# Two attention and expert layers on one core: the second layer's keys and values are projected during the first routing, its keys are split during the first experts, and the first attention masks and takes its row maxima on VectorE

## The reference

```python
x = x + attention(layernorm(x), ctx, ctx, mask, Wq, Wk, Wv, Wout, b_out, is_causal=1)
x = x + experts(layernorm(x), ...)            # 16 experts of width 512, the best 2 of each row
x = x + attention(layernorm(x), ctx, ctx, Wq, bq, Wk, bk, Wv, bv, Wo, bo)
x = x + experts(layernorm(x) * g + b, ...)    # 7 experts of width 1024, capacity 732, and a shared one

def attention(query, key, value, ...):        # 16 heads of 16 channels
    q, k, v = query @ Wq + bq, key @ Wk + bk, value @ Wv + bv
    scores = q @ k.T / 4                      # first layer only: causal and given mask set to -inf
    return softmax(scores) @ v @ Wo + bo
```

## Time and profile before

| | us |
|---|---|
| three runs | 1266.15, 1257.76, 1257.41 |
| median | 1257.76 |
| profiled execution: its time | 1257.77 |
| profiled execution: its span | 1256.0 |

### The profile page before, as it was taken

The page is one execution under the profiler, slowest core; times in us unless marked ns, Lnnn a source line. Parts: engine busy times, 40 slices in busy tenths (PEclk is TensorE's granted clock), DMA queues, the critical chain, the costliest instruction groups (busy, mean ns, idle before and its releaser), DMA issues. The chain is left out here.

```text
span 1256.0 us, 26319 instructions
## 1 busy us (share of the span) xinstructions
PE 1123.8 (89%) x8539; PEld 981.6 (78%) x8540; DVE 689.2 (55%) x1558; ACT 595.2 (47%) x1211; POOL 359.9 (29%) x502
## 2 busy tenths in 40 slices
PE   6999999729999984898998679999999999999997
PEld 4688787419999973565665379999999999999996
DVE  4755656562222236776776755555555555555556
ACT  3576666303233223776786344444444454444432
POOL 6556650112222215776531045000000000000251
PEclk9899999859999987999999779999999999999999
DMA  7775472665667848566580221223222232232132
GB/s 181 176 179 126 122 175 49 246 239 183 209 215 207 213 142 172 124 131 127 98 126 9 101 93 52 82 64 113 85 90 80 93 102 86 87 106 68 50 98 80
DMA packets 88713, 156.31 MB, mean 124 GB/s; under 512 B 11315, under 2 KB 60013, under 8 KB 87872
## 3 DMA queue, kind: packets, MB, share of 16 engines
q1 hardware_dynamic: 72288, 119.90, 36.5%
q0 software_dynamic: 9584, 29.32, 8.1%
q10 hardware_dynamic: 6768, 6.16, 1.5%
HBM read 116.86 MB, written 39.20 MB: 124 GB/s over the span
## 5 line engine op out<-in xcount | busy, mean ns | idle before, releaser
L2146 PE MATMUL e_ps<-xT_e,wp_e 128*128 128x384 f32 (+1 forms) x1344 | 245.2, 331 | 4.0 <-DVE wp_e L2020 4.0
L2146 PEld LDWEIGHTS e_ps<-xT_e,wp_e 128*128 128x128 f32 x1344 | 221.7, 188 | 5.4 <-issue 4.1
L640 DVE TENSOR_REDUCE att_ps<-att_ps 128x2 f32<-128x512 f32 (+1 forms) x224 | 155.2, 696 | 104.3 <-PE att_ps L987 64.5
L1978 ACT ACTIVATE act_a_e<-e_ps 128x256 f32<-128x256 f32 (+2 forms) x176 | 77.7, 442 | 159.0 <-PE e_ps L2146 153.9
L893 ACT ACTIVATE probs<-att_ps 128x384 f32<-128x384 f32 (+1 forms) x256 | 130.4, 546 | 43.2 <-PE att_ps L1019 28.9
L2076 DVE TENSOR_TENSOR hid_e<-act_a_e,e_ps 128x256 f32<-128x256 f32 (+2 forms) x176 | 86.9, 494 | 115.8 <-ACT act_a_e L1978 99.5
L1982 ACT ACTIVATE hidp_e<-hid_e 128x256 fp32r<-128x256 f32 (+2 forms) x176 | 83.8, 476 | 127.5 <-DVE hid_e L2076 119.7
L2163 PE MATMUL e_ps<-wp_e,hidp_e 128*128 128x256 f32 (+1 forms) x1008 | 138.4, 282 | 2.9 <-DVE xres L2036 1.2
L2078 DVE TENSOR_TENSOR hidp_e<-hid_e,hidp_e 128x256 fp32r<-128x256 f32 (+2 forms) x176 | 87.7, 498 | 95.4 <-ACT hidp_e L1982 91.6
L2163 PEld LDWEIGHTS e_ps<-wp_e,hidp_e 128*128 128x128 f32 (+1 forms) x1008 | 130.7, 183 | 4.9 <-issue 4.1
L1613 ACT ACTIVATE hid_e<-e_ps,b_ahead 128x128 f32<-128x128 f32 x188 | 53.6, 368 | 132.6 <-PE e_ps L1718 121.4
(11 more groups left out here) (236 smaller groups left out, 1855.1 us busy)
## 6 DMA issues: line engine op xcount, KB each, us to landing
w_e<-in_W SPq DMA_DIRECT2D x47, 512.0 KB
w_e<-in_W SPq DMA_DIRECT2D x57, 384.0 KB, 3.1
ks<-parts SPq DMA_DIRECT2D x96, 128.0 KB, 4.7
qs<-parts SPq DMA_DIRECT2D x96, 128.0 KB, 6.1
parts<-cut SPq DMA_DIRECT2D x30, 384.0 KB, 3.0
w_ahead<-in_W SPq DMA_DIRECT2D x4, 2048.0 KB, 17.9
x_e<-rows SPq DMA_DIRECT2D x8, 768.0 KB, 6.2
done<-y_e ACTq DMA_DIRECT2D x47, 128.0 KB, 1.9
```

Of the source, the lines that this page charges most:

```text
L640: dve.tensor_reduce(tops_at(at[3])[:, qt, x0:x0 + heads], src, AX.X, ALU.max).then_inc(reduced, 1)
L1978: act.activation(act_a[:, u % 2, 0:n], ps[:, AB + u % 2, 0:n], ACT.Silu).then_inc(silu_ready, 1)
L2146: last = pe.matmul(ps[:, bank + u % 2, 0:n], weights(lot, c, pw)[:, (b * DC + d) * P:(b * DC + d + 1) * P], xT[:, px, d, t0:t0 + n], start ...
```

## The change

Three parts.

1. **Attention 0.** `score` no longer adds the mask (8 matmuls a group fewer), and `scoreT` still does. On VectorE `reduce` becomes one `tensor_tensor_reduce` for each head: it adds the mask `shut` to the scores and takes the maximum of each row, 8 a group instead of 3 reductions; what it adds up is also written to a buffer that nobody reads. The maxima go to SBUF (`row_tops`), in both attentions. VectorE's loop over batches 1 to 4 is written out in attention 0.
2. **Keys and values of attention 1 for batches 2 to 7.** Routing 0 loads their context and the matrices, and projects batches 2, 3 and 4; experts 0 projects 5, 6 and 7, before and between its four lots and behind them. ScalarE takes each out of PSUM.
3. **Key parts.** GpSimd splits these keys during experts 0, one step between two gathers of rows, and stores the parts by its own DMA. In attention 1 batches 2 to 7 have no slots for keys and values, GpSimd splits queries only, and SP loads the key stack without a wait for a store and the query stack behind its own store. The loads `Wk`, `Wv` and `bk` go from experts 0 to routing 0.

The core of the diff:

```diff
+def project_early(pe, out, kv, f, kind, half):
+    ctx = kv["ctx"][:, f - OPENED]
+    for c in range(DC):
+        if kind == "k":
+            last = pe.matmul(out[:, half * S:(half + 1) * S], kv["wk"][:, c, half * P:(half + 1) * P], ctx[:, c, :], start=c == 0, stop=c == DC - 1)
+        else:
+            last = pe.matmul(out[:, half * D:(half + 1) * D], ctx[:, c, half * P:(half + 1) * P], kv["wv"][:, c, :], start=c == 0, stop=c == DC - 1)
+    return last
...
             def reduce(at, u):
                 qt, x0, heads = UNITS[u]
                 dve.wait_ge(scored, ready(group(at) * NU + u))
+                if causal:
...
+                    for x1 in range(heads):
+                        col = x1 * 512 // heads
+                        last = dve.tensor_tensor_reduce(out=closed_scores[:, qt, x0 + x1, 0:keys(qt)], in0=ps[:, unit_bank(at, u), col:col + keys(qt)],
+                                                        in1=shut[:, 0, at[0], qt, 0:keys(qt)], scale=1.0, scalar=MASKED, op0=ALU.add, op1=ALU.max,
+                                                        accum_out=tops_at(at[3])[:, qt, x0 + x1:x0 + x1 + 1])
+                    last.then_inc(reduced, 1)
+                    return
...
-                    last = pe.matmul(out, qs[0:KS, j, hd, qt * P:(qt + 1) * P], ks[0:KS, j, hd, 0:keys(qt)], start=True, stop=not causal)
-                    if causal:
-                        last = pe.matmul(out, m["identb"][:], closed(n, 0, qt, 0, keys(qt)), start=False, stop=True)
+                    last = pe.matmul(out, qs[0:KS, j, hd, qt * P:(qt + 1) * P], ks[0:KS, j, hd, 0:keys(qt)], start=True, stop=True)
...
             for f in range(FEED, B):
                 j = f % 2
                 for i, w in enumerate(KINDS):
-                    store(f, i, w)
+                    if not (kept and w == 1):
+                        store(f, i, w)
                 sp.wait_ge(scoredT, (f + 1) * H)
+                if kept:
+                    load_stack(sp, ks, j, parts_dram, 1, f, stacks_loaded[j])
+                    sp.wait_ge(parts_stored[j], stored_upto(f))
+                    load_stack(sp, qs, j, parts_dram, 0, f, stacks_loaded[j])
+                    continue
...
                 if fed(n):
-                    if ye is not None:
-                        split_stepwise(pool, f, 1)
-                    else:
+                    if not kept:
                         split(pool, f, 1)
...
+        IN_PICKS = ((2, "k", TB), (2, "v", TB + 1))
+        IN_RANKS = ((3, "k", WB), (3, "v", WB + 1), (4, "k", LB), (4, "v", LB + 1))
...
+                for c in range(DC):
+                    sp.dma_start(kv["ctx"][:, :, c, :], a["ctxT"][c * P:(c + 1) * P, OPENED * S:T].rearrange("p (f s) -> p f s", s=S)).then_inc(kv_loaded, 16)
+                for w in ("k", "v"):
+                    sp.dma_start(kv["w" + w][:], kv["W"]["W" + w].rearrange("(c p) n -> p c n", p=P)).then_inc(kv_loaded, 16)
...
-            for name in ("Wk", "Wv", "Wq", "Wo"):
+            for name in ("Wq", "Wo"):
...
             for n in range(NB0):
                 pool.wait_ge(turned, free(n))
                 pool.indirect_dma_start(x[:, n % RING], None, rows, bass.IndirectOffsetOnAxis(ap=owner[:, n:n + 1], axis=0)).then_inc(x_loaded[n % RING], 16)
+                k = n - RING
+                if 0 <= k < (B - OPENED) * (CUTS + 1):
+                    cut_keys(OPENED + k // (CUTS + 1), k % (CUTS + 1))
...
+            AT_LOT = (range(0, 4), range(4, 6), range(6, 7), range(7, 9))
             for k in range(2 * NT):
                 if k % MARKS == 0:
+                    for h in AT_LOT[k // MARKS]:
+                        make_half(h)
...
+            for h in range(AT_LOT[-1].stop, 2 * len(PIECES)):
+                make_half(h)
+            pe.wait_ge(kv_taken, len(PIECES) - 1)
```

More of the change, by code:

```diff
@@ L161, in attend_block @@
     biased = "bq" in W
+    kept = ye is not None
     ctx = ExitStack()
@@ L512, in values @@
             def values(n):
-                pool.wait_ge(v_taken, n + 1)
+                if not (kept and n >= FEED):
+                    pool.wait_ge(v_taken, n + 1)
                 if n >= 2:
@@ L795, in _ @@
                 split(dve, 1, 0)
-            batches(dve, batch)
+            if causal:
+                for n in range(B):
+                    batch(n, n % 2, n // 2, n == 0, n == B - 1)
+            else:
+                batches(dve, batch)
             normalize((B - 1, 1, None, NG - 1))
```

126 lines of the change are left out of this document (108 added, 18 removed).

## The result

The changed kernel takes 1250.3 us (median of six, 1244.75 to 1252.34), the kernel before, run beside it, 1259.2: a ratio of 0.993, with a 95% interval of 0.990 to 0.996. That is faster, but by 0.7% and not by the 2.4% predicted (1227.3 us), and above the range (1212 to 1248). The profiled execution took 1245.86 us, its span is 1244.2, against 1256.0 before.

The account below looks back on a forecast made before the run. It took TensorE to pace attention 0's projecting batches, with VectorE also near its limit in the last, and TensorE and GpSimd attention 1's. -7.5 - 21 - 3 + 1 = -30.5 us from 1257.77 gave 1227.3 us, range 1212 to 1248.

Parts of the forecast that it names:

- Attention 1, -21 us: Attention 1: without key and value projection and key split, batches come out at 20.8 us; -21 us (-25 to -15).
- Attention 0, -7.5 us: Attention 0: masks leave TensorE for VectorE's pairs; batches 1 to 5 save 9.5 us, batch 7 loses 2; -7.5 us.
- rival (b): Attention 0: VectorE's pairs are nearly free, 12 to 14 us gained; 1217 to 1222 us; chance 0.13.
- End of experts 0, -3 us: End of experts 0: three of eleven loads go, shortening TensorE's wait for weights and low clock; -3 us (-4 to -2).
- Routing 0 and start of experts 0, +1 us: Routing 0 and start of experts 0: twelve added 1.72 us pieces nearly fit idle time at full clock; +1 us (-1.5 to +8).
- rival (c): Routing 0: added pieces meet a low clock, its leave or the first lot waits, +8 us; 1234 us; chance 0.10.
- (d): Attention 1: query stacks stay its pace, a third of the 21 us or more is lost; 1235 to 1248 us; chance 0.08.
- (a): Attention 0: pairs cost VectorE the upper bound or more, gaining nothing or losing up to 6 us; 1234 to 1244 us; chance 0.20.

Follow-up runs that it names:

- e12: Changed kernel with a key split on parts nobody reads put back between last gather and bias in attention 1: 1254.1 us, ratio 0.994.
- e1: Changed kernel with GpSimd's roots and query split in attention 1 ordered by a semaphore instead of drains: 1240.9 us, ratio 0.987.
- e4: Kernel before with GpSimd's roots and query split in attention 1 ordered by a semaphore instead of drains: 1249.8 us, ratio 0.995.
- e5: Changed kernel with, in attention 1, GpSimd's roots and query split by semaphore and the row maxima in PSUM: 1237.0 us, ratio 0.985.
- e6: e5 with eight key matmuls put back in each feeding batch of attention 1, into a PSUM bank nobody reads: 1235.6 us, ratio 0.983.
- e2: Changed kernel with the row maxima of attention 1 back in PSUM, attention 0's still in SBUF: 1246.8 us, ratio 0.992.
- e14: Changed kernel with nothing else but the maxima of both attentions in PSUM: 1247.3 us, ratio 0.991.
- e9: Kernel before with unread matmuls around routing 0's last ranks and the lots, including six calls behind the last lot: 1258.6 us (one run).
- e13: e6 with VectorE's combines divided over groups 0 and 1 and attention 0's maxima in PSUM too: 1235.2 us, ratio 0.980.

## Why the prediction was wrong, step by step

**Attention 1, -21 us: wrong, 0 measured, and the whole miss.** Three sentences of that part fail.

- "GpSimd loses the key split ... 21.3 us a batch." The split was costed as work on a busy engine. It was the cover of a wait: GpSimd's drain doesn't end before its gathers have landed, and they land at the end of the stack loads. Measured, the batch of GpSimd is 26.1 to 26.2 us. The wait of 1.1 to 3.1 us at L393 was in the trace of before, directly below the rows that I cited the earlier trace rows, marked "issue"; I read it as a fixed cost:

```profile
542.29 0.18 POOL L393 CAST bits<-spread 128x2 f32<-128x2 int32 x1 [1.94 <-issue]
```

  e12 shows that 3.7 us of work more there are taken up by that wait (13.9 us of it become 3.1), e1 and e4 that the drains were the pace, worth 5.9 and 6.9 us of the stage.
- "TensorE needs 18.6 us a batch." True as a sum, useless as a pace. Group by group, keys lay where VectorE sets the pace, and values gave 0.78 us of 1.72 (both in batch 3). The comparison that isolates this term, e4 against e5 (both without the drain, both with maxima in PSUM), is 172.0 against 167.6 us: the whole early projection is worth 4.4 us in this stage, not 21.
- "the batch comes out at 20.8, above VectorE's need." Less work on TensorE brought its clock down to 0.87 to 0.93, as e6 shows by giving 1.0 us a batch back in group 1 for more matmuls. I had looked for low clock only in the stages where work was added, not where it was removed.

**Maxima in SBUF: missing.** The prediction describes the move and gives it no price. In attention 1 it is worth 5.5 us of the stage, 2.8 to 3.9 of the whole, once the drain is gone (e1 against e5), and 0.7 us of the stage, less than the scatter, with it (e2).

**Attention 0, -7.5 us: -7.5 measured, by luck: two errors cancel.** The pairs were put at 0.44 us each, 3.5 us a group. Their starts are 0.21 us apart for 128 columns and 0.35 for 256, which makes 4 x 0.21 + 4 x 0.35 = 2.2 us a group, hardly more than the 2.1 of the three reductions. The durations were right (285 and 420 ns for 292 and 428, 82 for 80), but the second half hides in the tail of the first, and the next pair starts ahead of its end; that is the lower bound of the prediction, rival (b). Three rows of the changed kernel's last batch:

```profile
198.93 0.28 DVE L683 CUSTOM_DVE_ANT_0 closed_scores<-att_ps,shut 128x128 bf16<-128x128 f32 x1
199.13 0.08 DVE L683 DVE_READ_ACCUMULATOR2_ANT row_tops<- 128x1 f32 x1
199.13 0.28 DVE L683 CUSTOM_DVE_ANT_0 closed_scores<-att_ps,shut 128x128 bf16<-128x128 f32 x1
```

So the last two batches got shorter (20.3 to 18.9 and 18.24 to 17.48) where nothing and 2 us more were predicted. Against it, batches 1 to 5 average 23.2 and not 22.4 us, 5.3 us less in all and not 9.5. Some 0.35 us a batch are the stalls behind GpSimd, net of the dearer second instructions (e14). In the rest TensorE is busy 21.9 us (a need of 21.6 was predicted) and idles for 0.7 us in short gaps, with VectorE at 16.7. That points to TensorE's order within the group as the pace, and not the sum of either engine; no run shows it.

**End of experts 0, -3 us: right.** TensorE's wait for weights is 0.83 us (436.08) instead of the 1.98 of the earlier trace rows, the low clock behind it is gone (16 matmuls in 2.02 us instead of 2.68), and from the second expert to the end it is 3.0 us less.

**Routing 0 and start of experts 0, +1 us: -2.2 measured.** The pieces fit, and the clock was full behind them: the first 32 matmuls take 3.74 instead of the 5.32 of the earlier trace rows. The prediction had that gain as "up to 1.4 us", and it came in full (e9: 1.6 to 1.8), while of the cost that it was set against (2.4 us) nothing is left at the end. A small part of rival (c) did happen: the pieces ahead of the first lot met half clock for 3.4 us from 257.3 and took 5.2 us instead of 3.4, and the first lot came 0.6 us later (38.2 us behind the start of routing 0 instead of 37.6). By the last lot that was made up.

**Start of attention 1, not in the sum: +1.3 us,** with half clock for 20.5 us from 465.5 and 10.2 from 489.4, where it was 13.7 us from 485.7 before. It is within the scatter of other executions (40.9 us on the mean of the changed ones, 40.7 before), so it asks for no cause.

Of the rivals, (d) had the right stage, nearly the right time (1235 to 1248) and most of the mechanism: the query stacks stayed the pace. What it lacked is why GpSimd was late with the queries' parts: not 21.3 us of work, but a drain that waits for gathers behind those same stack loads. Its 0.08 was too low for a part that carried two thirds of the forecast on three engines at once. Two of the rivals' ranges are wider than their own terms: (b), 12 to 14 us off attention 0, makes 1221 to 1223 us and not 1217, and (a), nothing to +6, makes 1235 to 1241 and not 1244. The measured terms are -7.5 - 2.2 - 3.0 + 1.3 + 0 - 0.5 = -11.9 us against -30.5 predicted. Of the 18.6 us between them attention 1 is 21, and the other terms give 2.4 back. (The medians differ by 8.9 us, less than the two profiled executions, since that of the changed kernel was one of its fast ones.)

## What to carry to other kernels

Before an operation is costed as saved, look at the first wait behind it on its engine: if that wait ends at an event that the operation doesn't cause, the saving only makes it longer. Where an engine's work is light and its batch is long, follow the ring of waits through the queues once around, SP's included. Sum an engine's work by group of the schedule and not by batch, and count a matmul as saved only in the groups where TensorE itself is the last to be ready; elsewhere it may be what keeps the clock up. Order GpSimd's small steps behind software gathers by semaphores rather than by drains. VectorE's small operations on PSUM don't stall beside GpSimd, which pays only where VectorE is in the pace (e5 against e1, but not e2, e13 or e14).

## What the runs showed of the hardware

- With gathers still in flight, the step behind a drain on GpSimd starts 0.29 us after the last of them has landed (556.73 and 556.44 us; before, 542.29 and 542.00). So it is in 26 drains of nine kernels, and the idle time in them is up to 6.6 us. Ordered by a semaphore the next step starts after 0.07 us, with gathers that land up to 5.5 us later.
- VectorE's operations of 0.17 us with all inputs in SBUF took up to 2.12 us beside an elementwise operation of GpSimd. The same operations with the maxima in PSUM took 0.17 each time.
- Eight key matmuls more in a batch whose clock was 0.93 made it 0.9 and 1.1 us shorter, with the clock at 1.00 (e5 and e6, batches 2 and 3).
- A `tensor_tensor_reduce` from PSUM costs 0.21 us for 128 columns and 0.35 for 256 from start to start (medians), with the maximum going to SBUF, and 0.25 and 0.35 with it going to PSUM (0.24 and 0.35, 0.27 and 0.37 on the mean; second instruction 82 and 147 ns).
